# A layer of expert mixing, state-space scan and expert mixing again on one core: the opening of the scan stage is rearranged, and part of its gathers is issued in the stage before

## The reference

```
def _ffn(x, gate_w, experts):            # E = 8 experts, M = 2048 / 8 = 256 tokens for each
    gates = sinkhorn(einsum('bnd,de->bne', x, gate_w))        # 8 rounds of normalising
    vals, idx = top_k(swapaxes(gates, -1, -2), M)             # each expert picks its M tokens
    routed = x[b_idx, routed_indices]
    outputs = einsum('ebmd,edf->ebmf', routed, experts) * gate_values
    return zeros_like(x).at[b_idx, routed_indices].set(outputs)   # the last expert wins

def _mixer(x, ...):                      # 512 inner channels, 16 states, convolution of 4 taps
    x_ssm, res = split(x @ W_in.T)
    x_conv = silu(conv(x_ssm) + conv_b)
    delta  = softplus(x_conv);  A_d = exp(delta[..., None] * A)
    h_t = A_d * h_(t-1) + x_conv * x_conv          # along the 2048 tokens
    y = x_conv * sum(h_t over 16 states) * silu(res) + D * x_conv
    return y @ W_out.T

x = x + 0.5 * _ffn(layernorm(x));  x = x + _mixer(layernorm(x), ...);  x = x + 0.5 * _ffn(layernorm(x))
```

## Time and profile before

| what | value |
|---|---|
| median of three runs | 3874.86 us (3873.5 to 3882.03) |
| the profiled execution | 3868.75 us, span 3867.2 us |
| busy: PE, VectorE, ScalarE, POOL | 2728.7, 3147.4, 2131.2, 1277.2 us |
| share of the span | 71%, 81%, 55%, 33% |
| VectorE busy, 1200 to 2500 us | 1262.1 of 1300 us |
| VectorE busy, 430 to 560 us | 26.9 of 130 us |
[...]

### The profile page before, as it was taken

How to read it: one execution, slowest core, us unless ns; L and a number is a source line. 1 busy time by engine, 2 the same in 40 slices (tenths; PEclk the granted TensorE clock), 3 DMA queues, 4 the chain that set the end, 5 groups by cost and what they waited for, 6 DMA issues and landing times. The chain is left out here.

```text
span 3867.2 us, 27624 instructions
## 1 busy us (share of the span) xinstructions
PE 2728.7 (71%) x8204; PEld 1465.5 (38%) x8204; DVE 3147.4 (81%) x2562; ACT 2131.2 (55%) x2282; POOL 1277.2 (33%) x896
## 2 busy tenths in 40 slices
PE   8300288799889889989989978987896691016553
PEld 4200143346345445444534634543442450014442
DVE  5799239999999999999999999999999467972222
ACT  5300257876887787688687687678666171001111
POOL 0000336344344534634624534440110100006665
PEclk9655689999999999999999999999998895558766
DMA  6200437778778868877877777876775561015667
GB/s 257 109 3 0 136 75 163 178 167 166 171 160 173 193 140 177 182 155 161 182 163 170 159 175 170 171 171 122 146 135 115 117 258 46 0 47 172 219 215 239
DMA packets 146914, 576.14 MB, mean 149 GB/s; under 512 B 22192, under 2 KB 73968, under 8 KB 99952
## 3 DMA queue, kind: packets, MB, share of 16 engines
q0 software_dynamic: 77568, 402.71, 50.2%
q1 hardware_dynamic: 69232, 172.11, 12.2%
HBM read 154.72 MB, written 117.51 MB: 70 GB/s over the span
## 5 line engine op out<-in xcount | busy, mean ns | idle before, releaser
L1035 DVE TENSOR_TENSOR_SCAN state<-state,drive 128x2048 f32<-128x2048 f32 x512 | 2220.9, 4406 | 76.2 <-ACT state L1200 76.2
L1200 ACT ACTIVATE state<-delta,neg_a 128x2048 f32<-128x2048 f32 x512 | 1019.9, 2002 | 276.9 <-DMA state<-state 188.9
L1371 PE MATMUL ps_states<-state,ident 128*128 128x512 f32 x1800 | 903.2, 649 | 169.4 <-DMA state<-state 169.1
L931 POOL DMA_DIRECT2D state<-state x256 | 232.7, 911 | 1292.1 <-DVE state L1035 1281.4
L1371 PEld LDWEIGHTS ps_states<-state,ident 128*128 128x128 f32 x1800 | 364.5, 209 | 613.3 <-issue 401.9
L1307 PE MATMUL ps_proj<-x1t,w_in 128*128 128x512 f32 x1024 | 500.2, 625 | 72.4 <-ACT conv_in L1116 54.9
L1323 PE MATMUL ps_proj<-conv_in,tap 128*128 128x512 f32 x1024 | 456.9, 594 | 0.8 <-ACT conv_in L1116 0.5
L879 POOL DMA_INDIRECT picked<-normed_rows,slot_now x128 | 368.6, 2880 | 254.0 <-DVE gate_now L973 187.7
L895 POOL DMA_INDIRECT x<-routed_rows,row_now x128 | 330.2, 2580 | 155.1 <-issue 64.6
L1307 PEld LDWEIGHTS ps_proj<-x1t,w_in 128*128 128x128 f32 x1024 | 195.7, 197 | 339.4 <-issue 235.7
L1323 PEld LDWEIGHTS ps_proj<-conv_in,tap 128*128 128x128 f32 x1024 | 191.7, 189 | 245.7 <-issue 245.0
(11 more groups left out here) (255 smaller groups left out, 3252.0 us busy)
## 6 DMA issues: line engine op xcount, KB each, us to landing
state<-state POOLq DMA_DIRECT2D x256, 1024.0 KB, 7.7
delta<-xc POOLq DMA_DIRECT2D x24, 1024.0 KB, 11.9
normed_rows<-rows_in SPq DMA_DIRECT2D x8, 2048.0 KB, 7.4
expert<-in_experts SPq DMA_DIRECT2D x64, 256.0 KB
routed_rows<-routed SPq DMA_DIRECT2D x128, 128.0 KB
x<-in_x POOLq DMA_DIRECT2D x16, 1024.0 KB, 10.9
x_rows<-x SPq DMA_DIRECT2D x16, 1024.0 KB, 7.8
x_rows<-rows_out POOLq DMA_DIRECT2D x64, 256.0 KB, 8.7
```

Source lines behind the costliest of these rows:

```text
L931: nc.gpsimd.dma_start(out=state[held(q)][:], in_=state[held(q - 1)][:], accum_op=ALU.add).then_inc(pair_landed(b, q // 2)[0], 16)
L1035: nc.vector.tensor_tensor_scan(state[held(q)][:], state[held(q)][:], drive[j % 2][:], 0.0, ALU.mult, ALU.add).then_inc(state_ready, 1)
L1200: nc.scalar.activation(state[held(q)][:], delta[j % 2][:], ACT.Exp, scale=g.neg_a[:, j, n:n + 1]).then_inc(decay_ready, 1)
L1371: mm = nc.tensor.matmul(ps_sum[c][:], g.ident[:], state[held(q)][:, c * CH:(c + 1) * CH], start=(opening and n == 1), stop=(n == N - 1))
```

## The change

- In both selections `slot_token` is computed first, and POOL then issues the first eight gathers of batch 0 (`HEAD`) into `early_rows`. This buffer is allocated for the whole kernel: it is also the mixer's `state0`, and the last stage's `picked` buffers.
- In the mixer's opening, the slots of batch 0 and of batch 1 (32) are made one after the other. Their gathered rows lie in state0, state1, delta0, delta1, their products in state2, state3, xc2, xc3, and all eight experts are loaded at once into xc0 and xc1. Nothing there is used twice. Batch 1's products go to the second `routed_rows` table.
- Batch 0's gathers back go to state4 and state5; x is loaded into x1 by SP, and VectorE adds pairs of tiles (`join`). No accumulating DMA of x, and the normalised rows go to state0 and state1. Four rows and half of the copies of x1t are made on VectorE.
- Silu reads the convolution's PSUM directly, chunk by chunk; delta is completed by a VectorE add, not by a DMA. ScalarE makes six decays (`AHEAD`) between and before the copies of the other chunks.
- The body of batch 0 has no slots of batch 1 any more.
- The tables are set anew; the diff shows those that the prediction speaks of and some neighbours.
- After the mixer its semaphores are cleared, with a barrier.

```diff
+        pool.wait_ge(slots_set, 1)
+        for s in range(HEAD):
+            nc.gpsimd.indirect_dma_start(
+                out=g.early[:, s * D:(s + 1) * D], out_offset=None, in_=g.normed,
+                in_offset=bass.IndirectOffsetOnAxis(ap=g.slot_token[:, 0, s:s + 1].bitcast(U32), axis=0)
+            ).then_inc(g.early_in[tag][s], 16)
...
-    SET = 38
+    SET = 35
-    BACK = 14
+    BACK = 15
-    STATS = (28, 35)
-    COPY_OUT, ADD_OUT = (9, 11, 12, 16, 19, 20, 22, 24), (7, 9, 13, 15, 15, 21, 21, 23)
-    PUT_OUT = (1, 3, 5, 7, 11, 13, 15, 17)
-    BEGIN = (7, 7, 7, 7)
-    GATE, COMBINE = (3, 3, 4, 4), (6, 5, 6, 4)
+    STATS = (27, 36)
+    COPY_OUT, ADD_OUT = (9, 11, 12, 16, 17, 19, 22, 24), (7, 11, 13, 15, 15, 19, 23, 25)
+    PUT_OUT = (1, 3, 5, 9, 11, 13, 15, 17)
+    BEGIN = (7, 8, 8, 8)
+    GATE, COMBINE = (3, 3, 4, 4), (6, 4, 6, 4)
-    STEP = {9: 1, 27: 2, 41: 3, 59: 4}
+    STEP = {9: 1, 27: 2, 43: 3, 59: 4}
-    SCALE = (30, 38)
+    SCALE = (29, 38)
...
-    state = [sb(f"state{i}", [P, NT]) for i in range(NF + NC)]
+    state = [g.early] + [sb(f"state{i}", [P, NT]) for i in range(1, NF + NC)]
...
+    PICKED = (state[0], state[1], delta[0], delta[1])
+    ROUTED = (state[2], state[3], xc[2], xc[3])
+    BROUGHT, NORMED = (state[4], state[5]), (state[0], state[1])
+    ON_ACT = T - 4
+    AHEAD = 6
+    GROUP = (0, 0, 1, 2, 3, 4, 6)
...
-        ("res", 1): (24, 25, 25, 26),
+        ("res", 1): (25, 25, 26, 27),
...
+        for e in range(E):
+            sp.dma_start(early_expert(e), g.experts[e].rearrange("(k p) f -> p k f", p=P)).then_inc(early_expert_in, 16)
+        for i in range(2):
+            sp.dma_start(x1[:, i * TH:(i + 1) * TH, :], x_v[0, :, i * TH:(i + 1) * TH, :]).then_inc(early_x_in[i], 16)
...
+        def join(p):
+            i = 2 * p // TH
+            if 2 * p % TH == 0:
+                dve.wait_ge(early_x_in[i], 16)
+            dve.wait_ge(early_back_in[p], 2 * 16)
+            rows = x1[:, 2 * p:2 * p + 2, :].rearrange("p t d -> p (t d)")
+            at = 2 * p % TH * D
+            nc.vector.tensor_tensor(rows, rows, BROUGHT[i][:, at:at + 2 * D], ALU.add).then_inc(x1_joined, 2)
...
+        dve.wait_ge(soft_done, 1)
+        nc.vector.tensor_tensor(delta[0][:], delta[0][:], xc_now[0], ALU.add).then_inc(early_step, 1)
...
+                act.wait_ge(conv_done, c + 1)
+                nc.scalar.activation(xc_now[0][:, c * CH:(c + 1) * CH], ps_proj[c % 2][:], ACT.Silu, bias=g.conv_b[:, 0:1]
+                                     ).then_inc(conv_copied, 1)
...
+        soft_exp(0, 0)
+        chunk_read(*rest[0])
+        soft_log(0, 0)
+        chunk_read(*rest[1])
+        square(0, 0)
+        for q in range(AHEAD):
+            decay(0, q, True)
+            for chunk in rest[2 + GROUP[q]:2 + GROUP[q + 1]]:
+                chunk_read(*chunk)
...
+        nc.clear_and_free_semaphores(nc.allocated_since(held))
+        nc.all_engine_barrier()
```

More of the change, by code:

```diff
@@ L805, in at_slot @@
     def at_slot(v, start, end, first, more, last):
-        if first and 0 <= v - FIRST_FFN < end:
-            return 1, v - FIRST_FFN
         if not last and not first and v + J * N >= start and (v + J * N - start) % 2 == 0 and (v + J * N - start) // 2 < end:
@@ L840, in body @@
         def body(b, first, more, last):
-            if first:
-                for i in range(2):
-                    sp.wait_ge(x_in[i], (b + 1) * 16)
-                    sp.sem_inc(g.passed_sp, 1)
-                load_expert(b + 1, 0)
-                load_expert(b + 1, 1)
             for s in range(SL):
-                if not last and (first or s >= EARLY):
+                if not (first or last) and s >= EARLY:
                     store_slots(b + 1, s)
@@ L924, in body @@
         def body(b, first, more, last):
-            if first:
-                for s in range(NX + 4 - FIRST_FFN):
-                    pick(b + 1, s)
             for q in range(1, J * N, 2):
@@ L940, in body @@
                     continue
-                for v in (q, q + 1):
-                    if first and NX <= v < SL + FIRST_FFN - 4:
-                        pick(b + 1, v + 4 - FIRST_FFN)
                 if not first or q >= PICK:
@@ L1233, in body @@
                         square(*((b, j + 1) if j < J - 1 else (b + 1, 0)))
-        for s in range(SL + 1):
-            if s < SL:
+        for s in range(2 * SL + 1):
+            if s < 2 * SL:
                 act.wait_ge(pick_turned, s + 1)
@@ new lines, in copy_early @@
+        def copy_early(i):
+            act.wait_ge(x1_turned, i + 1)
+            nc.scalar.copy(x1t[:].rearrange("p k (n t) -> p t k n", t=T)[:, 2 * i:2 * i + 2],
+                           ps_rows[i % 2][:].rearrange("p (t k n) -> p t k n", t=2, k=KD)).then_inc(early_copied[0], 1)
+        deviation(0, 0)
+        act.wait_ge(shift_done, 1)
+        for t in range(TH):
+            normalise_early(t)
+        copy_early(0)
+        copy_early(2)
+        deviation(0, 1)
+        act.wait_ge(shift_done, 2)
@@ L1263, in _ @@
+        act.wait_ge(conv_copied, C)
+        both_tables()
+        rest = opening[last_conv + 1:]
+        soft_exp(0, 0)
[7 more added lines that the diff above has]
+                chunk_read(*chunk)
+        for chunk in rest[2 + GROUP[AHEAD]:]:
+            chunk_read(*chunk)
         batches(act, body)
@@ L1312, in project_ssm @@
             u = b * J + j
[L1313 to L1314 removed]
+            if c == 0 and not (isinstance(b, int) and b == 0):
+                pe.wait_ge(x1t_copied, b * G2)
             pe.wait_ge(*bank_user("ssm", b, j, c))
```

292 lines of the change are left out of this document (175 added, 117 removed).

## The result

| kernel and place | before, us | with the change, us | ratio, 95% interval |
|---|---|---|---|
| the measurement that the prediction was made for, 10 runs of each | 3877.6 | 3853.69 (3842.65 to 3866.99) | 0.9941 [0.9928, 0.9954] |
| a later session (`after_again`) | 3816.48 | 3758.37 (3756.99 to 3762.99) | 0.985 [0.9834, 0.9867] |

What follows compares the result with a forecast made beforehand. VectorE's scans set the mixer's time; its opening, a serial chain, is the largest wait. 39.5 + 10 + 15 + 4 - 1 = 67.5 us off 3868.75 gives 3801, 3807 for the median; range 3788 to 3822.

Steps and rivals of the forecast that it cites:

- the slots' pace: Mixer's opening, 32 slots: three at 2.1 us, the rest at 1.25, so slot 31 is scaled at 451.4.
- First product: Mixer's opening: PE's first expert product waits for all eight expert loads, at 408.3 where it was 406.97; 1.3 us lost.
- Selection's gathers: Eight gathers beside 16 compares in each selection: take 19 us of 29 left, end before 390, cost VectorE 0.
- Rival C: Both selections: POOL's gathers hold up VectorE's compares, 15 us lost, 3822; chance 0.04.
- Chunk to scan: Mixer's opening, from the last convolution chunk to VectorE's first scan: 10.2 us, giving the first scan at 500.7.
- Batch 0: Batch 1's slots and gathers leave this batch, so VectorE's waits for late decays shrink: 10 us gained, bounds 0 and 16.
- Steady: Seven steady batches: new tables cut VectorE's waits before combine 0 and the gate; 15 us gained, from -10 to 33.
- Rival A: Steady batches: tables give nothing or take a little, -10 to 5, while opening and batch 0 gain: 3817 to 3832; chance 0.20.
- rival D: Steady batches: later step 3 eats ScalarE's lead, decay 48 comes last on VectorE; 3875 and slower; chance 0.04.
- Costs: Clearing the mixer's semaphores and the barrier after it: 0 to 6 us, 1 taken.
- Last stage: Its first eight gathers are made ahead in the second selection: gain 0 to 11 us, 4 taken.
- Rival B: Mixer's opening: PE's clock stays at 0.50, first scan at 526, gain 14 in place of 39.5, so 3833; chance 0.08.

Runs made afterwards that it cites:

- after_again: The kernel after, unchanged, run again in a later session beside the kernel before: 3758.37 us (ratio 0.985), no halts in its trace.
- e7: Kernel after with first x1t transpose copies back at position 37, step 3 at 41, last two convolution chunks of unit 3 at 39: 3756.04 us (0.9855).
- e8: Kernel after with opening slot gathers 2.2 us apart, first transpose copies at 37, last stage's first eight gathers issued there: 3839.48 us, kernel before 3876.84.

## Why the prediction was wrong, step by step

- *The step that failed is the slots' pace*, "a pace of 1.6 for the later slots" its worst bound, and the gathers that "wait for nothing". Where there are no halts the pace was 1.084 us (1.25 taken), and slot 31's scaling ended at 445.04 (451.4). With halts it ended at 480.76, since the slots stood still twice, for 19 us and for 17. That put the first scan at 532.31 in place of 500.7, and the time, 3853.69, outside the forecast. The sum's two paces are steps of the trace of before: 2.1 is 406.97 to 409.11, with PEclk at 0.50, and 1.25 half of 419.94 to 422.46; without halts the first three scalings stood 2.13 and 1.77 apart (from 409.44). The range had no room for 35 us, since I read the pace from 16 slots whose gathers waited for them and not from the last stage, where the halts stood. What brings the halts stays open. In a session without halts this step was sound, and the 58 us measured there missed the 67 by the smaller terms below.
- *First product* 408.3: 407.36 and 407.72. *Selection's gathers* ending before 390 and VectorE losing nothing: the last was issued at 381.41, and the compares took 18.26 against 18.25. Rival C falls: no run shows VectorE held up by them, nor the 15 us. Of the eight gathers five took 1.97 to 2.01 us and one 2.88 (0.95 alone), so it is POOL's instructions that get longer.
- *Gathers back* from 434.1 to 452.8: 431.00 to 450.27. *x1t ready* 466: 464.4. *Projection to last convolution chunk* 24.4: 23.1 (and 24.7 with halts). The 1 for a slower clock was my estimate: PEclk over this stretch was 0.92 before, 0.93 in `after_again` and 0.87 with halts. *Chunk to scan* 10.2: 10.0 in both. The last two are right in both kinds, to 1.5 us; gathers back and x1t are only without halts, to 3.1 us.
- *Batch 0*: 10, measured 6.7 and 7.5. The wait at scan 6 was 3.43 and 1.73, and a second of 1.96 follows it; 2.2 was taken for both.
- *Steady*: 15, measured 6.7 and 5.3. Combine and gate gave 2.8 + 3.0 us in batch 2, above their bound of 4.7, and the term went to the late decays. Rival A, whose tables give 5 at most, was nearer for this term than the forecast. What I left out is that the table that moved copies one position earlier set ScalarE waiting for PE. I named rival D's place wrongly: decay 48 is never late, decays 42 to 44 are, and the later step 3 that D blames is, together with the two convolution chunks, a gain (e7). D's price, a microsecond a batch costs seven, was right.
- *Costs* 1: 1.65 and 0.5 for clear and barrier. `route` itself came out 1.05 shorter once and 3.4 longer once. The gathers in it aren't the reason: e8, without them in the second `route`, took as long (388.92). *Last stage* 4: 4.6 without halts, from one trace of the kernel before (345.3); 16 of kernels with the eight gathers made ahead lie from 339.5 to 344.4. With halts it can't be told.
- *Rival B* (first scan at 526) comes within 6 us of the first scan with halts but isn't what happened: between the halts PEclk is 0.92, and `after_again` has 0.98 from 412 to 432. The windows with 0.52, 0.66 and 0.67 are those in which PE was busy for only 4.28 of 7, 4.93 of 20 and 5.95 of 19 us.

## What to carry to other kernels

Before counting on dense gathers beside a short chain, look in the trace for a stage that has both, and for idle time whose releaser is "remote" or "issue". No dependency that the trace shows as open explains it, and here more such overlap brought more of it (34 us put down to these two from the first product on among the slots of the kernel after, none before the change). Where it stands, see whether the trace has the landings of its transfers at all (here 14854 updates of 20576); if not, the recording itself is a suspect. A copy placed one step earlier than its data sends the wait to whatever is queued behind it (3.0 us at position 36, 0.7 at 37); in a table of positions, check each number against the producer's end. And a bound taken from a stage in which requests wait for each other says nothing on one in which they don't.

## What the runs showed of the hardware

In some sessions ScalarE, and in the last stage VectorE too, stand idle for up to 11.6 and 8.5 us at a time although the work that they wait for is recorded as done, while GpSimd issues indirect gathers 1.25 us apart. Where the trace has the update that releases them, that update is late, by 12 and 17 us in the two cases of the opening. With 2.2 us between the gathers the 32 slots of the opening ran in such a session without it (one run). It costs 35 us in the opening (532.31 against 497.50) and some 60 in the last stage (403.5 against 340.6). All ten runs of such a session have the longer time, and in other sessions it is absent. What differs between the sessions, and whether plain transfers would do the same, stays open.

The traces with halts lack most records of landings where engines stand still (28 against 576 from 412 to 432 us, 688 against 4223 from 3480 to 3700); from 1200 to 1500 us, where neither halts, the counts are 1531 and 1616. So records are lost somewhere on their way, and mostly in these places. That the loss and the halts have one cause, so that the halts are a cost of recording, is my guess from these counts alone; no run shows it: each run here has a span and a granted clock on record, so each was recorded, and there is no time without recording to set beside these. Until there is one, the 61 us between the kinds of session, and the 35 us of the opening, may not be the kernel's own.
